# A fused transformer layer on one core: batch 0's linear-attention parts go straight from SBUF to the stacks, a weight wait moves, and a token table is begun earlier

## The reference, cut to what matters

```python
x = L0_attn_x                                    # 8 batches x 512 tokens x 128
mod = (silu(L0_c) @ L0_wmod)                     # sa, ca, ga, sb, cb, gb per batch
h = layernorm(x) * (1 + ca) + sa
# linear attention, 16 heads of 8
q, k, v = split(h @ Wqkv.T + bqkv)
q = (elu(q) + 1 + 1e-4) / sqrt(8);  k = elu(k) + 1 + 1e-4
num = q . cumsum(k v);  den = q . cumsum(k) + 1e-4
x = x + ga * layernorm((num / den) @ Wout.T + bout, gamma, beta)
h = layernorm(x) * (1 + cb) + sb
# ffn block on h: softmax attention (16 heads), then a mixture of 8 experts, one per token by argmax
h = h + softmax_attention(layernorm(h)) @ w_proj
out = h + expert[argmax(layernorm(h) @ gate_w + gate_b)](layernorm(h))
x = x + gb * out
```

## Time and profile before

| | us |
|---|---|
| median of three runs | 714.31 |
| profiled execution, its own time | 713.35 |
| its span, first to last instruction | 711.2 |
| PE busy | 635.7 (89%) |
| DVE busy | 613.3 (86%) |
| ACT busy | 494.0 (69%) |
| POOL busy | 413.6 (58%) |
| mean granted PE clock | 0.960 of full |

### The profile page before, as it was taken

One profiled execution on the slowest core, in us unless ns is written; L12 is line 12 of the kernel. 1 busy time (PEld: TensorE's weight loads), 2 busy tenths in 40 slices (PEclk: granted clock), 3 DMA queues, 4 the chain that ended last, 5 costly groups with the idle time before them and its releaser, 6 DMA issues.

```text
span 711.2 us, 16640 instructions
## 1 busy us (share of the span) xinstructions
PE 635.7 (89%) x5448; PEld 329.8 (46%) x5448; DVE 613.3 (86%) x1568; ACT 494.0 (69%) x1007; POOL 413.6 (58%) x929
## 2 busy tenths in 40 slices
PE   4498789889888789899999999999999999799994
PEld 2276566666555412122333333333323323498994
DVE  6868999998978898889999999999999994676552
ACT  3534555766654438788888888888888889755662
POOL 4122465575574565144766787887777771566553
PEclk9789999999999959999999999999999999999998
DMA  6663142351352412116430120302103000465600
GB/s 180 150 243 128 53 135 76 105 178 63 118 179 90 134 45 91 45 45 180 149 90 1 40 86 13 113 24 77 48 21 105 25 12 35 121 183 173 175 31 12
DMA packets 42341, 67.05 MB, mean 94 GB/s; under 512 B 7965, under 2 KB 35584, under 8 KB 39057
## 3 DMA queue, kind: packets, MB, share of 16 engines
q1 hardware_dynamic: 38480, 56.73, 25.9%
q0 software_dynamic: 3296, 8.41, 3.3%
q10 hardware_dynamic: 480, 0.85, 0.5%
HBM read 43.22 MB, written 23.04 MB: 93 GB/s over the span
## 4 chain that ended last, share of the span: by engine, by line
PE 46%; DVE 24%; ACT 12%; POOL 8%; issue 7%; SPq 1%; DMA 0%; ACTq 0%; POOLq 0%; DVEq 0%
DVE arena L1545 11%; PE bank L1056 8%; ACT arena L1974 6%; PE pair L1307 5%; PE pair L1045 5%; PE bank L1017 4%; DVE arena L1378 3%; PE bank L1316 2%; PE pair L1316 2%; POOL arena L695 2%; DVE arena L1407 2%; PE bank L902 2%; ACT arena L1943 2%; PE bank L913 2%; PE bank L887 2%
## 5 line engine op out<-in xcount | busy, mean ns | idle before, releaser
L1974 ACT ACTIVATE arena<-pair 128x512 f32<-128x512 f32 x506 | 278.1, 603 | 50.4 <-PE pair L1045 48.4
L1545 DVE TENSOR_REDUCE arena<-bank 128x1 f32<-128x512 f32 x388 | 251.3, 682 | 7.1 <-PE bank L1017 6.1
L1045 PE MATMUL pair<-q_stack,k_stack 64*128 64x512 bf16 x506 | 158.0, 386 | 5.8 <-ACT arena L1974 5.1
L1017 PE MATMUL bank<-k_stack,q_stack 63*128 63x512 bf16 x388 | 137.4, 396 | 8.8 <-DVE arena L1545 5.0
L1056 PE MATMUL bank<-arena,values 128*9 128x512 f32 x1024 | 134.4, 597 | 1.6 <-ACT arena L1974 1.5
L1378 DVE TENSOR_TENSOR arena<-bank,cst 128x512 f32<-128x512 f32 x128 | 82.2, 683 | 15.6 <-PE bank L887 14.9
L1545 DVE TENSOR_REDUCE arena<-pair 128x1 f32<-128x512 f32 x124 | 84.2, 679 | 1.5 <-PE pair L1017 1.1
L1017 PEld LDWEIGHTS bank<-k_stack,q_stack 63*128 63x128 bf16 x388 | 33.3, 93 | 109.3 <-DVE arena L1545 24.9
L695 POOL TENSOR_TENSOR arena<-arena 128x32 f32<-128x32 f32 (+6 forms) x312 | 68.4, 219 | 24.4
L1045 PEld LDWEIGHTS pair<-q_stack,k_stack 64*128 64x128 bf16 x506 | 40.6, 93 | 48.3 <-ACT arena L1974 26.2
L1890 ACT ACTIVATE arena<-bank,den_eps 128x512 f32<-128x512 f32 x32 | 21.7, 678 | 43.1 <-PE bank L913 43.1
(11 more groups left out here) (299 smaller groups left out, 1261.7 us busy)
## 6 DMA issues: line engine op xcount, KB each, us to landing
linear_parts<-arena SPq DMA_DIRECT2D x8, 768.0 KB, 3.7
q_stack<-linear_parts SPq DMA_DIRECT2D x48, 128.0 KB, 2.9
softmax_parts<-arena SPq DMA_DIRECT2D x8, 768.0 KB, 4.1
q_stack<-softmax_parts SPq DMA_DIRECT2D x48, 128.0 KB, 2.9
k_stack<-softmax_parts SPq DMA_DIRECT2D x48, 128.0 KB, 2.9
k_stack<-linear_parts SPq DMA_DIRECT2D x42, 128.0 KB, 2.9
arena<-in_L_ffn_w_dram SPq DMA_DIRECT2D x16, 256.0 KB, 4.5
v_all<-token_rows SPq DMA_DIRECT2D x20, 192.5 KB, 2.7
```

The lines of the kernel that those rows point to most:

```text
L1017: pe.matmul(bank[:], qs[b % 2][rows, slot, qt * P:(qt + 1) * P], ks[b % 2][rows, slot, :], start=True, stop=True).then_inc(d_s_m, 1)
L1045: pe.matmul(score_bank(s)[:], ks[u][rows, 2 * g + x, kt * P:(kt + 1) * P], qs[u][rows, 2 * g + x, :], start=True, stop=True).then_inc(d_s_ ...
L1545: dve.reduce_max(mx[:, m % 2, col:col + 1], bank[:], AX).then_inc(d_s_mr, 1)
L1974: act.activation(pt[:, kt % 2, x, half, :], score_bank(s)[:], ACT.Exp, scale=SCALE).then_inc(d_s_e, 1)
```

## The change

It makes five edits.

1. For batch 0, no store and no loads through DRAM: SP issues twelve `load_stack_direct` copies from `a_parts` to the stacks, six when the first parts are ready, four at the second, two at the third. They stand ahead of `small_loads`. ACT issues none. ACT's `a_first_part(1, ...)`, which overwrites `a_parts`, now waits for all twelve; for later batches it waits for the store of the batch before, whose count is one lower now.
2. The stacks of index 1 are cleared by POOL (in steps -3 and -2, slot 3) and not by DVE.
3. PE's wait for `SETUP` moves from the slot of `products(0)` to `project(0)`, and the output weights are turned into a corner of `bank[4]`, not `bank[0]`.
4. DVE's `masked(0)` moves ahead of batch 1's two `a_rest`.
5. The early table's first part is done in group 30, `kt` 3, the other two in group 31 as before; ACT's `d_numerators_out(31)` moves ahead of its wait for the table.

```diff
+def load_stack_direct(eng, k, parts, u, side, i, loaded):
+    dst = (k.ks if side else k.qs)[u][i:P:PRODUCTS]
+    part = 3 * side + (KEY_PART if side else QUERY_PART)[i]
+    eng.dma_start(dst.rearrange("p s l -> p (s l)"), parts[:, part, :]).then_inc(loaded, 16)
@@ SP
+                sp.wait_ge(w_s_z, 2)
+                for part in range(3):
+                    for side in range(2):
+                        if part == 0:
+                            sp.wait_ge(a_s_p1, side + 1)
+                        elif part == 1:
+                            sp.wait_ge(a_s_p2, side + 1)
+                        else:
+                            sp.wait_ge(a_s_p3, 2)
+                        for i in range(6):
+                            if (KEY_PART if side else QUERY_PART)[i] == part:
+                                load_stack_direct(sp, k, a_parts, 0, side, i, k.s_stk[0])
                 small_loads(nc, sp, k, w_s_sm)
...
-                        sp.wait_ge(a_s_p3, 2 * a + 2)
-                        store_parts(sp, k.linear_dram[a], a_parts, a_s_ps)
+                        if a:
+                            sp.wait_ge(a_s_p3, 2 * a + 2)
+                            store_parts(sp, k.linear_dram[a], a_parts, a_s_ps)
+                            sp.wait_ge(a_s_ps, 16 * a)
+                            wait(sp, s_at, NL * (a - 1))
+                            sp.wait_ge(w_s_z, 4)
+                            for load in STACK_LOADS:
+                                load_stack(sp, k, k.linear_dram, a % 2, a, *load, k.s_stk[a % 2])
@@ POOL
                                 a_rstd(s + 3)
+                            if s < -1:
+                                pool.wait_ge(w_s_z, s + 5)
+                                pool.memset((ks, qs)[s + 3][1][:].bitcast(F32), 0.0).then_inc(w_s_z, 1)
@@ PE
                 def project(q):
+                    if q == 0:
+                        pe.wait_ge(w_s_v, SETUP)
...
-                            pe.transpose(k.bank[0][:, 3 * P:4 * P], wo_pos, k.ident).then_inc(w_s_t, 1)
+                            pe.transpose(k.bank[4][:, P:2 * P], wo_pos, k.ident).then_inc(w_s_t, 1)
                         if s == -1 and d == NL - 1:
-                            pe.wait_ge(w_s_v, SETUP)
@@ DVE
-                            cleared(1)
...
                             a_feature(s + 2, 1)
+                            if s == -1:
+                                masked(0)
                             a_rest(s + 2, 0)
...
-                        if kt == 1 and n == NB - 1:
+                        if kt == 3 and n == NB - 2:
                             at = dispatch_at(EARLY - 1) + C * NE
                             dve.wait_ge(d_s_fe, C * EARLY + 3)
-                            for part in range(3):
-                                table(False, d_ot[:, 2, at:at + NE], part)
+                            table(False, d_ot[:, 2, at:at + NE], 0)
+                        if kt == 1 and n == NB - 1:
+                            table(False, None, 1)
+                            table(False, None, 2)
@@ ACT
                     act.wait_ge(a_s_ph, 2 * a + z + 1)
-                    wait(act, a_s_ps, 16 * a)
+                    if a == 1:
+                        act.wait_ge(k.s_stk[0], N_STACK)
+                    wait(act, a_s_ps, 16 * (a - 1))
...
-                            if s == -1:
-                                act.wait_ge(a_s_ps, 16)
-                                act.wait_ge(w_s_z, 2)
-                                for load in STACK_LOADS[1::2]:
-                                    load_stack(act, k, k.linear_dram, 0, 0, *load, k.s_stk[0])
...
+                d_numerators_out(NB - 1)
                 act.wait_ge(d_s_ta, 1)
                 weights(0)
-                d_numerators_out(NB - 1)
```

More of the change, by code:

```diff
@@ L544, in _ @@
                             sp.dma_start(k.mod_dram.rearrange("i b d -> b i d"), mrow).then_inc(w_s_md, 16)
-                        sp.wait_ge(a_s_ps, 16 * (a + 1))
-                        wait(sp, s_at, NL * (a - 1))
-                        sp.wait_ge(w_s_z, 2 if a == 0 else 4)
-                        for load in STACK_LOADS if a else STACK_LOADS[0::2]:
-                            load_stack(sp, k, k.linear_dram, a % 2, a, *load, k.s_stk[a % 2])
-                        if a == 0:
                             sp.wait_ge(w_s_md, 16)
@@ L1718, in gate_bias @@
                                       ).then_inc(d_s_gb, 1)
-                def cleared(u):
-                    for stack in (ks, qs):
-                        dve.memset(stack[u][:].bitcast(F32), 0.0).then_inc(w_s_z, 1)
-                cleared(0)
+                for stack in (ks, qs):
+                    dve.memset(stack[0][:].bitcast(F32), 0.0).then_inc(w_s_z, 1)
                 for s in STEPS:
@@ L1727, in _ @@
                         g = s * NL + d
-                        if unit(g):
+                        if unit(g) and g:
                             masked(g)
```

2 lines of the change are left out of this document (1 added, 1 removed).

## The result

The changed kernel took 708.34 us (median of 5 runs, 706.94 to 709.66), against 714.31 (713.6 to 716.53) for the kernel before: a ratio of 0.9909 with a 95% interval of [0.9893, 0.9925]. 709.1 was forecast. The profiled execution took 706.94, its span is 705.1 at a mean granted clock of 0.970 (before 713.35, 711.2 and 0.960).

The account below looks back on a forecast made before the run. One long chain through PE, DVE and ACT sets the end, so the starts of linear attention and experts matter. 713.35 - 3.3 (head) - 1.4 (end) = 708.65, plus half of 0.96: 709.1 us; range 705.8 to 712.6.

Parts of the forecast that it names:

- The copies: SP's twelve batch 0 copies, limited by issue at 0.65 us each: SP free at 26.3, stack 0 landed at 28.65.
- Rivals 3 and 4: SP's batch 0 copies up to 1.5 times slower, 710.5, chance 0.14; under half the loads' rate, 722 at a third, chance 0.07.
- Two late things behind one wait: Before the first unit, stack 0, output weights' copy and DVE's chain end late together; removing the weight wait alone leaves 0.3 us.
- The first unit: First linear attention unit on PE starts at about 29.8 behind PE's own queue, 5.5 us early; state sum near 1.7 us.
- The wait for stack 1: PE waits 2.2 us before the ninth unit for stack 1, landing at 55.9; 3.3 us of the head's gain is left.
- 2.0 to 2.7 early, I take 2.5: SP's broadcast of the modulations goes out at 32.3 to 33.0, not 34.98; later SP work moves by the same.
- PE then waits for ACT's norm: In the first units, PE waits for ACT's norm of batch 2; second and third units still about 5.5 us early.
- wrong if the ninth unit waits for no DMA: Sign at PE's ninth unit, near 56: without a wait for a stack load there, the prediction counts as wrong.
- POOL's memsets: Two added POOL memsets of 1.8 us, near 8.2 to 10.0 and 15.6 to 17.4; no cost to DVE taken.
- The end: At the experts' start, PE's first turn comes 1.9 us earlier, ACT's table load 1.0; 1.4 us taken as gain.
- rival 2: The head's gain is given back in the linear stage, only the end's is left: 712.4 us, chance 0.12.
- rival 1: Full head gain, by quicker SP issues or engines making good the wait: 5.5 + 1.9 off, 706.5 us, chance 0.17.

Follow-up runs that it names:

- e3: Memsets on POOL, PE's weight wait at the projection and first mask ahead of the rests, on the kernel before, without direct copies: 714.89 us, ratio 1.0005.
- e4: Only the direct copies of batch 0, added to the kernel before: 714.97 us, ratio 1.0002.
- e2: The changed kernel with the early table and last-sums edit at the experts' start taken back: 710.28 us, ratio 0.9945.
- e10: The changed kernel with SP's eight projection loads moved behind batch 1's stack loads: 708.55 us, ratio 0.9913.
- e12: The changed kernel itself, measured and profiled once more in another session: 709.11 us, ratio 0.9919 to the kernel before.
- e11: The changed kernel with SP's projection loads behind batch 1's stack loads and 16 unused PE transposes before batch 2's turn: 706.54 us, ratio 0.9887.
- e7: The changed kernel with 16 unused PE transposes in the idle 1.85 us before batch 2's turn: 721.34 us, ratio 0.9912 in a slower session.
- e8: The changed kernel with batch 2 normed first, DVE masks earlier and SP's projection loads behind batch 1's stack loads: 721.88 us, ratio 0.9936, slower session.
- e9: The changed kernel with batch 2 normed first on ACT and DVE masks earlier, SP's row unchanged: 724.19 us, ratio 0.9946, slower session.
- e1: Only the early table and last-sums edit at the experts' start, added to the kernel before: 712.61 us, ratio 0.9973.
- e13: e11 with the broadcast of the modulations behind batch 1's loads and POOL's wait moved to its first use: 707.42 us, ratio 0.9898.

## Why the prediction was right, point by point

**The copies, right.** The issue rate is the limit, as forecast: 12 x 0.65 = 7.8 us, SP free at 26.0 (forecast 26.3), stack 0 complete at 28.0 (28.65). Rivals 3 and 4, a slow copy between partitions, fell: the landing of 2.4 to 2.6 us is shorter than that of loads from DRAM. At the issue rate the copies move 1.57 MB in 7.8 us, 202 GB/s. That is below the 218 GB/s that the Trainium skill, SBUF — State Buffer, section "Door 1: The DMA port swizzle", gives for 8 ports, so no run here shows whether its limit would bind if they were issued faster.

**Two late things behind one wait, right.** The forecast saw stack 0, the copy of the weights and the chain behind that copy late together, and said that with the weight wait alone gone the stack would leave 0.3 us. e3 and e4 show it with nothing for either; e2 has 3.9 us for both.

**The first unit, right**: 29.06 for 29.8, with PE's queue and no wait ahead of it, and the state sum at 1.74 us and clock 1.00. PE's rows ahead of it had also become 0.55 us earlier (28.86 for 29.41).

**The wait for stack 1, right in kind and length, the head 0.6 to 1.1 us too small.** This is the mis-sized term. The ninth unit was forecast at 55.9; it starts at 54.84 in one execution, 55.32 in another and 55.20 in e2, so the head is worth 3.9 to 4.4 and not 3.3. The step that was off is the broadcast "2.0 to 2.7 early, I take 2.5". I took 0.4 us for the modulations' store and 2.3 to 3.0 for its landing, from rows of 128 KB; this store has 20 KB and the broadcast follows 1.69 us after its issue (29.52 to 31.21). The broadcast was 3.3 to 3.8 early (31.21 and 31.69 for 34.98), and the last load of stack 1 2.8 to 3.8 (51.54 and 52.55 for 55.38). That SP's row decides holds for this kernel: the store leaves where the row lets it and takes the 3.7 us that it took before. It is not the only thing there: behind the row stands the broadcast in the DMA engines, and the store that left 4.1 us earlier in e10 landed at 44.41, where e12's lands at 44.36. With the row alone shortened the store lands 0.05 (e10), 0.8 (e11 against e7) and 1.55 us (e8 against e9) earlier, though it leaves 3.1 to 4.1 earlier.

**What the forecast didn't have.** PE waits 1.85 us for ACT's norm of batch 2. The wait was named ("PE then waits for ACT's norm") and not priced, and in one of two executions some 3 us near half clock follow it. It cost next to nothing only because stack 1 comes behind it: with the drop the fourth unit is 1.6 us later than without (40.67 and 39.06), and the ninth is not (54.84 and 55.32). So the condition "wrong if the ninth unit waits for no DMA" came true in the first profile, and would have refuted a right mechanism; e2 and e12 show the wait, of 1.70 and 2.32 us for 2.2 forecast.

**POOL's memsets, right.** Two of 1.81 us, at 8.17 and 15.35. The Trainium skill, SBUF — State Buffer, section "Who interferes with whom", would have a DVE copy or tensor_scalar in a two-port mode wait under them. No such wait shows: beside the second memset DVE's relu took 0.75 us at 16.10, as long as at 14.88 without it. But that is no test of the rule: every DVE copy and tensor_scalar under either memset reads PSUM (`bank`, `pair`), and one from SBUF to SBUF beside a memset of POOL was not measured.

**The end, right in place; its size, 1.4, lies between the two that the traces show.** First turn 1.80 earlier behind the last sums (1.9 forecast), ACT's table load 0.87 (1.0). At the end of the span 0.93, 1.08 (e12) and 0.78 (e1) are left; 1.4 was taken as a middle between the two, and against this profile of the kernel before it is 0.5 too large: ACT's row was the end to take, since the last projection waits for ACT (L2164). But that profile is the one of four without edit 5 in which PE kept its clock at the experts' start; against the other three the end is worth 2.0 to 3.3 us, and the runs of e1 say 1.9 [0.9, 3.0]. The forecast has no term for this clock.

**Given back later (rival 2), no.** From the ninth unit to the last mask pair it is 176.55 us before, and 175.75, 176.72 and 176.90 in the changed kernel, in e12 and in e2. The gain is carried through. Full gain (rival 1) needed the wait for stack 1 to vanish; e13 does that and the head is then worth 59.24 - 53.78 = 5.5 us, but 177.06 us follow. In the traces the two errors in size nearly cancel: 4.7 was forecast for head and end, 3.9 + 1.1 = 5.0 and 4.4 + 0.9 = 5.3 were measured. That the runs gain 6.5 us, where 5.2 was forecast between the medians, fits the clock at the experts' start. So it is in part luck that 709.1 lies as close to 708.34 as it does. Between single executions the two long stages in the middle add their own scatter: e12's softmax stage (last mask pair to last sums) took 376.42 us, 0.93 more than before, the linear stage of the first execution 0.80 less.

**What stays open.** Why the clock drops after the same idle time in one execution and not in another, and how often it does at the experts' start. Why e11 (706.54) and e13 (707.42), which differ little in their traces, are below e12 by 2.6 and 1.7 us when their ninth units are only 1.2 and 1.5 earlier; their linear stages vary by as much with the clock.

## What to carry to other kernels

When an engine stands before a wait for several things, list all that end near it, and price an edit by the second latest: parts that measure nothing alone may be worth their whole gain together. When work is issued earlier, ask what fills the DMA engines at that moment: a store issued 4 us earlier behind a broadcast of 2.5 MB landed at the same time. And when one profile lacks a wait that the sum forecast, take a second execution before the mechanism is dropped. The same holds for the profile that a change is measured against: here the one profile of the kernel before kept a clock that three others lost.

## What was not expected of the hardware

- Copies from SBUF to SBUF, 128 KB each from 128 partitions to 16 partitions eight apart, land in 2.4 to 2.6 us (medians; the longest 2.8), less than the 2.9 to 3.0 of loads of the same size from DRAM to the same places.
- A store of 20 KB was followed by its reader 1.69 us after its issue, one of 768 KB 3.7, and the same one 5.3 to 7.8 where a broadcast of 2.5 MB had been issued 4.7 to 6.3 us ahead of it.
- After an idle stretch of 1.85 us PE was granted 0.50 for three microseconds in one execution, and 1.00 after 1.84 us in another of the same kernel. It dropped after a wait for stack 1 of 1.24 us in e8, 2.54 in e9 and 2.52 in e10, and not after one of 1.70 in e2 and 2.32 in e12. At the experts' start it dropped behind 2.47 to 2.67 us (e2, e3, e4) and 0.87 us (e9), and not behind 2.67 us in the kernel before.
